# A graph network's first edge sweep: selections built from widened rows on TensorE, ScalarE and VectorE in place of products on VectorE and GpSimd

## The reference, cut to what matters

```python
xj = x[dst]                          # a row for each edge
s, v = xj[:, :64], xj[:, 64:]
msg  = linear(s, v)                  # plain
     + dist * mix(s, v)              # weighted by the fourth attribute
     + sum over i of r_vec[i] * mix_i(s, v)
agg  = segment_sum(msg, src)         # by the other end of the edge
x    = layernorm(x + x + bilinear(x, agg) + linear(x))
```

## Time and profile before

| | |
|---|---|
| median of 3 runs | 7056.59 us (7055.1 to 7059.43) |
| profiled execution, first to last instruction | 7384.0 us |
| sorting | to about 115 us |
| the first layer's sweep over the edges | about 115 to 2,482 us |
| first layer's node steps with the second layer's messages | about 2,500 to 5,410 us |
| second layer's node steps | to the end |
| busy over the whole span | PE 80%, PEld 64%, DVE 75%, ACT 51%, POOL 75% |

### The profile page before, as it was taken

One profiled execution on the slowest core, in us unless ns is written; L12 is line 12 of the kernel. 1 busy time (PEld: TensorE's weight loads), 2 busy tenths in 40 slices (PEclk: granted clock), 3 DMA queues, 4 the chain that ended last, 5 costly groups with the idle time before them and its releaser, 6 DMA issues.

```text
span 7384.0 us, 145782 instructions
## 1 busy us (share of the span) xinstructions
PE 5898.2 (80%) x52295; PEld 4739.6 (64%) x52295; DVE 5535.0 (75%) x7299; ACT 3742.5 (51%) x11578; POOL 5548.6 (75%) x4491
## 2 busy tenths in 40 slices
PE   5666666666666588888898989988849999999999
PEld 3444444545544477777776777777737777777777
DVE  5666666767666577777777777777728999998888
ACT  2232322323232355555555555555527777777776
POOL 3787877788878567777777777777757888888887
PEclk6777777777777799999999999999969999999999
DMA  7877777777776366776776777677632222222222
GB/s 219 244 229 223 230 218 224 224 225 232 224 221 194 107 203 229 234 234 222 232 242 223 239 237 228 227 236 231 211 118 93 94 94 94 94 94 95 95 96 75
DMA packets 681151, 1381.01 MB, mean 187 GB/s; under 512 B 106047, under 2 KB 487661, under 8 KB 654447
## 3 DMA queue, kind: packets, MB, share of 16 engines
q1 hardware_dynamic: 527695, 1090.23, 46.7%
q0 software_dynamic: 152736, 281.45, 11.3%
HBM read 587.20 MB, written 784.08 MB: 186 GB/s over the span
## 4 chain that ended last, share of the span: by engine, by line
PE 50%; DVE 13%; issue 12%; ACT 11%; another core or an unknown queue 8%; POOL 3%; SPq 1%; DMA 1%; DVEq 0%; POOLq 0%; ACTq 0%
PE node_ps L1373 13%; PE prods_ps L1341 5%; PE prods_ps L1322 5%; ACT onehot L1722 4%; PE prods_ps L1325 3%; DVE zs L1054 3%; PE node_ps L1390 3%; PE m_ps L1238 2%; PE s_ps L1238 2%; PE m_ps L1390 2%; POOL slots L649 2%; PE turn_ps L1360 2%; PE s_ps L1220 2%; PE node_ps L1238 2%
## 5 line engine op out<-in xcount | busy, mean ns | idle before, releaser
L649 POOL DMA_INDIRECT slots<-pay,slot_all x3136 | 3282.2, 1047 | 905.8 <-issue 835.5
L1722 ACT ACTIVATE onehot<-node_iota,msgs 128x125 f32<-128x125 f32 x3400 | 1030.2, 397 | 75.4 <-POOLq L711 75.4
L1373 PEld LDWEIGHTS node_ps<-msgs,onehot 128*125 128x125 f32 x6800 | 931.9, 188 | 149.3 <-issue 108.8
L1373 PE MATMUL node_ps<-msgs,onehot 128*125 128x160 f32 x6800 | 980.6, 303 | 45.8 <-ACT onehot L1728 32.7
L1104 DVE TENSOR_REDUCE upd<-work 125x48 f32<-125x3072 f32 x300 | 1003.9, 3346 | 6.9
L1091 DVE TENSOR_TENSOR work<-prods_ps,yv 125x1024 f32<-125x1024 f32 x800 | 930.9, 1216 | 35.6 <-PE prods_ps L1326 24.5
L1220 PE MATMUL s_ps<-ident,picks_sb 128*125 128x128 f32 x1568 | 377.2, 383 | 574.8 <-issue 486.3
L751 POOL TENSOR_TENSOR q<-xt,yv 125x3072 f32<-125x3072 f32 x100 | 547.7, 5477 | 339.6 <-PE turn_ps L1360 323.0
L1238 PE MATMUL m_ps<-win,picks_sb 125*128 125x160 f32 x3136 | 673.5, 343 | 104.7 <-issue 62.5
L724 POOL TENSOR_TENSOR q<-xt,yv 125x512 f32<-125x512 f32 x400 | 428.3, 1073 | 383.9 <-PE turn_ps L1360 360.7
L1220 PEld LDWEIGHTS s_ps<-ident,picks_sb 128*125 128x125 f32 x1568 | 306.4, 271 | 621.3 <-issue 610.2
(11 more groups left out here) (274 smaller groups left out, 14481.9 us busy)
## 6 DMA issues: line engine op xcount, KB each, us to landing
msgs<-slots SPq DMA_DIRECT2D x200, 1428.0 KB, 6.4
slots<-zero SPq DMA_DIRECT2D x183, 1386.0 KB
win<-table SPq DMA_DIRECT2D x784, 160.0 KB
picks<-picks_sb SPq DMA_DIRECT2D x196, 512.0 KB
picks_sb<-picks SPq DMA_DIRECT2D x196, 512.0 KB
table<-tab SPq DMA_DIRECT2D x200, 350.0 KB
slots<-pay,slot_all POOLq DMA_INDIRECT x3136
spill_in<-spill_sums SPq DMA_DIRECT2D x200, 80.0 KB, 6.0
```

Of the source, the lines that this page charges most:

```text
L649: g.indirect_dma_start(out=slots[layer][:, :], out_offset=bass.IndirectOffsetOnAxis(ap=slot_all[:, j:j + 1], axis=0), in_=pay[q][:, j - UB ...
L1373: te.matmul(node_ps[0:HM, 0:D], onehot[:, j, :], msgs[b][:, j, 0:D], start=(j == 0), stop=False)
L1722: last = ac.activation(onehot[:, j, :], node_iota[:, :], ACT.Square, bias=msgs[b][:, j, LOCAL:LOCAL + 1], scale=-1.0)
```

## The change

For each edge there are two rows now in SBUF, laid out with the edges along the free axis: the five weights (1, `dist`, r0, r1, r2; partitions 0 to 4 of `so.rows`) and `REL` (partition 32). `widen` multiplies them by constants, so that both appear on 125 partitions: `channel` (5 x 125) repeats each weight for the 25 nodes in `weight_ps`, a row of ones repeats `REL` in `s_ps`. ScalarE copies the weights to SBUF (`widened`), and one VectorE operation compares `REL` with the partition's own node and multiplies by the weight (`select`). The result is the turned selection itself, in `pick_n`; the transposes, `pick_out`, `weigh` and VectorE's two former operations are gone. All this is done one unit ahead, in halves of 4 blocks, and `select` stands within `rank_unit`, once in each half.

The attributes as rows are a new input (`attr_rows`, turned on the host); `REL` is turned piece by piece (`turn_rel` on TensorE, `keep_rel` on ScalarE), stored (`put_rel`), and loaded for each chunk (`load_rows`). The first layer's table matmuls now write to `turn_ps` and the second half of `prods_ps[1]`, since its first half holds the widened weights; `first_table` waits for `t_out` for that.

```diff
@@ sync @@
+            def put_rel(pc, groups, blocks):
+                sp.wait_ge(piece_out, 3 * pc + 3)
+                e0 = pc * PIECE * P
+                sp.dma_start(rel_d[e0:e0 + groups * blocks * P].rearrange("(g q e) -> q g e", q=blocks, e=P),
+                             so.rel_t[0:blocks, 0:groups, :]).then_inc(rel_put, 16)
             def load_recs(layer, k):
...
-                    if layer == 0:
-                        sp.wait_ge(s["picked"], 4 * c - 4)
-                        sp.wait_ge(s["weighed"], 4 * c - 4)
+            def load_rows(k):
+                c, ck, cb = k
+                if within(c, 2, NCH):
+                    sp.wait_ge(LS[0]["widened"], 4 * c - 4)
+                e0, n = c * CB * P, min(CB * P, E - c * CB * P)
+                sp.dma_start(so.rows[cb][1:CHANNELS, 0:n], attr_rows[:, e0:e0 + n]).then_inc(rows_in[cb], 16)
+                sp.dma_start(so.rows[cb][32:33, :].rearrange("p (a e) -> p a e", a=CB),
+                             rel_d[e0:e0 + CB * P].rearrange("(p a e) -> p a e", p=1, a=CB)).then_inc(rows_in[cb], 16)
...
             load_recs(0, (1, 0, 1))
+            sp.wait_ge(rel_put, 16 * (FULL + 1))
+            load_rows((0, 0, 0))
+            load_rows((1, 0, 1))
...
-                    sp.wait_ge(LS[0]["pick_out"], 4 * c + 2 * hh + 2)
+                    sp.wait_ge(LS[0]["picked"], 4 * c + 2 * hh + 2)
...
                 if within(c, 0, NCH - 2):
+                    load_rows(later(later(k)))
                     load_recs(0, later(later(k)))
@@ gpsimd @@
-            def weigh(k, hh, part):
...
             def chunk(k):
-                c, ck, cb = k
                 for hh in range(2):
-                    for part in range(2):
-                        if within(c, 0, NCH - 1):
-                            weigh(later(k), hh, part)
-                        scatter(0, k, hh, PAIRS // 2 * part, PAIRS // 2 * part + PAIRS // 2)
+                    scatter(0, k, hh)
@@ vector @@
-            def select(layer, k, hh):
...
+            def select(u, part):
+
+                c, hh, i = u // 2, u % 2, 2 * u + part
+                s, o = LS[0], UB // 2 * P * part
+                ve.wait_ge(s["wide_out"], i + 1)
+                if part == 0 and u >= 2:
+                    ve.wait_ge(s["msg"], 4 * u - 4)
+                    ve.wait_ge(picks_kept[hh], 16 * c)
+                ve.scalar_tensor_tensor(pick_n[hh][0:WROWS, o:o + UB // 2 * P], s_ps[0:WROWS, 0:UB // 2 * P], win_node[0:WROWS, :],
+                                        wide[part][0:WROWS, :], ALU.is_equal, ALU.mult).then_inc(s["picked"], 1)
...
                     link(ve.tensor_reduce(so.rank[:, hh, COUNT_COLS * pb:COUNT_COLS * (pb + 1)], pick, AX_X, ALU.add))
+                    if u + 1 < UNITS:
+                        select(u + 1, pb)
...
                     rank_unit(k, hh)
-                    if within(k[0], 0, NCH - 1):
-                        select(0, later(k), hh)
@@ tensor @@
+            def turn_rel(pc, groups, blocks):
+                te.wait_ge(edge_made, pc + 1)
+                rel = so.edge[:, :, :, :].rearrange("p c k f -> p (c k) f")[:, :, REL]
+                for g in range(groups):
+                    mm = te.transpose(s_ps[0:blocks, P * g:P * g + P], rel[:, blocks * g:blocks * g + blocks], ident[:, :])
+                mm.then_inc(turned_e, 1)
...
-            def turn_pick(layer, k, hh, part):
...
+            def widen(u, part):
+
+                c, hh, i = u // 2, u % 2, 2 * u + part
+                cb, s = c % 2, LS[0]
+                if i % 4 == 0:
+                    te.wait_ge(rows_in[cb], rows_first[cb] + 32 * (c // 2) + 32)
+                if i > 0:
+                    te.wait_ge(s["picked"], i)
+                o, n = UB * P * hh + UB // 2 * P * part, UB // 2 * P
+                te.matmul(weight_ps[0:WROWS, 0:n], channel[:, :], so.rows[cb][0:CHANNELS, o:o + n], start=True, stop=True)
+                te.matmul(s_ps[0:WROWS, 0:n], ones_f[32:33, 0:WROWS], so.rows[cb][32:33, o:o + n], start=True, stop=True
+                          ).then_inc(s["widened"], 1)
...
                 for hh in range(2):
-                    turn_pick(0, k, hh, 0)
+                    ahead = 2 * c + hh + 1
                     count(4 * c + 2 * hh + 1, 1)
-                    turn_pick(0, k, hh, 1)
                     messages(0, k, hh, 0, both)
+                    if ahead < UNITS:
+                        widen(ahead, 0)
                     if hh == 1 and made:
                         first_table(tile_of(k), 1)
                     messages(0, k, hh, 1, both)
...
                     messages(0, k, hh, 2, both)
+                    if ahead < UNITS:
+                        widen(ahead, 1)
                     messages(0, k, hh, 3, both)
@@ scalar @@
+            def keep_rel(pc, groups, blocks):
+                ac.wait_ge(turned_e, 2 * pc + 2)
+                if pc > 0:
+                    ac.wait_ge(rel_put, 16 * pc)
+                ac.copy(so.rel_t[0:blocks, 0:groups, :], s_ps[0:blocks, 0:groups * P].rearrange("q (g e) -> q g e", e=P)).then_inc(piece_out, 1)
...
-            def pick_out(layer, k, hh, part):
...
+            def widened(u, part):
+                i, s = 2 * u + part, LS[0]
+                ac.wait_ge(s["widened"], i + 1)
+                if i >= 2:
+                    ac.wait_ge(s["picked"], i - 1)
+                ac.copy(wide[part][0:WROWS, :], weight_ps[0:WROWS, 0:UB // 2 * P]).then_inc(s["wide_out"], 1)
...
                 for hh in range(2):
-                    pick_out(0, k, hh, 0)
-                    pick_out(0, k, hh, 1)
+                    ahead = 2 * c + hh + 1
                     located(0, k, hh)
                     pay_out(0, k, hh, 0, both)
+                    if ahead < UNITS:
+                        widened(ahead, 0)
...
                     pay_out(0, k, hh, 2, both)
+                    if ahead < UNITS:
+                        widened(ahead, 1)
                     pay_out(0, k, hh, 3, both)
```

More of the change, by code:

```diff
@@ L66 @@
 Q_MULS = (4, 1)
-MINE = 4
 DIRECT = (3, 2)
@@ L96, in layer_scales, with build @@
                 u_sv=(S * V) ** -0.5, u_vs=(S * V) ** -0.5)
-def build(nc, x, src, dst, attr, weights, out):
+def build(nc, x, src, dst, attr, attr_rows, weights, out):
     N = x.shape[0]
@@ L191, in build @@
         pick_n = pick_b[0:2]
-        pick_e = [z[:, 0:UB * WROWS].rearrange("p (j n c) -> p j n c", j=UB, c=CHANNELS) for z in pick_b[2:4]]
+        wide = [pick_b[2][:, z * UB // 2 * P:(z + 1) * UB // 2 * P] for z in range(2)]
         pay = [sb(f"pay{q}", [P, UB, ROW]) for q in range(4)]
@@ L246, in build @@
         so.zeros = sb("zero_rows", [P, ZERO * D], F32, early)
+        so.lane_i = sb("lane_i", [P, WIN], I32, early)
+        so.lane = sb("lane", [P, WIN], F32, early)
+        so.channel_i = sb("channel_i", [CHANNELS, WROWS], I32, early)
+        so.rel_t = pick_b[0][:, 0:PIECE].rearrange("q (g e) -> q g e", e=P)
+        so.rows = [z[0:33, :, :].rearrange("p g e -> p (g e)") for z in so.attr]
         early.close()
@@ L279, in build @@
             sem(z) for z in ("floats", "turned_e", "piece_out", "keyed", "based", "spread", "edge_made", "edge_put"))
+        rel_put = sem("rel_put")
+        rows_in, rows_first = piece_in[0:2], [48 * ((FULL + 1 - b) // 2) for b in range(2)]
         hot, counted, ranking, placed = sem("hot"), sem("counted"), sem("ranking"), sem("placed")
@@ L295, in layer_sems @@
                 s[n] = sem(f"{n}_l{layer}")
-            for n in (("picked", "weighed", "pick_turned", "pick_out"), ("copied", "mixed_mul"))[layer]:
+            for n in (("widened", "wide_out", "picked"), ("copied", "mixed_mul"))[layer]:
                 s[n] = sem(f"{n}_l{layer}")
@@ L971, in chunk @@
                     scale([(0, 1), (1, 0), (1, 1)])
-            ve.wait_ge(consts, 3)
+            ve.wait_ge(consts, 4)
             bucket_rows(0, 0)
-            select(0, (0, 0, 0), 0)
-            select(0, (0, 0, 0), 1)
+            for b in range(2):
+                one = ve.memset(so.rows[b][0:1, :], 1.0)
+            one.then_inc(consts, 1)
+            select(0, 0)
+            select(0, 1)
             chunk_sweep(ve, chunk)
@@ L1209, in count @@
                 mm.then_inc(counted, 1)
-            def turn_pick(layer, k, hh, part):
-                c, ck, cb = k
-                s = LS[layer]
-                te.wait_ge(s["picked"], 4 * c + 2 * hh + 2)
-                te.wait_ge(s["weighed"], 4 * c + 2 * hh + 2)
-                if within(2 * c + hh + part, 1, 2 * UNITS):
-                    te.wait_ge(s["pick_out"], 4 * c + 2 * hh + part)
-                for j in range(UB // 2):
-                    mm = te.transpose(s_ps[0:WROWS, P * j:P * j + P],
-                                      pick_e[hh][:, UB // 2 * part + j, :, :].rearrange("p n c -> p (n c)"), ident[:, :])
-                mm.then_inc(s["pick_turned"], 1)
+            def widen(u, part):
[9 more added lines that the diff above has]
```

(20 more changed lines are left out.)

79 lines of the change are left out of this document (36 added, 43 removed).

## The result

The changed kernel takes 7750.81 us (median of 4 runs) against 7058.01 us for the kernel before, measured beside it: a ratio of 1.098 (95% interval 1.0965 to 1.0996). It is 693 us slower; the prediction said 7300 us with a range up to 7620.

A forecast was written before the change was run, and what follows sets the result against it. GpSimd (POOL) was taken as the bound at 12.06 us a unit. Afterwards the ring, 2 x 4.40 + 2.00 = 10.8, plus 2.28 and 0.2 for the clock, gives 13.3; over 196 units +243 us, 7300 us (range 6880 to 7620).

The forecast's parts named there:

- What bounds the kernel now: First layer's edge sweep: GpSimd's scatters and `weigh` products fill 12.06 us a unit; removing the products saves 1.33 us.
- The ring: Each half unit: `bucket_rows`, `count`, `messages`, `widen`, copy, `select` and hand-overs in a row, 4.40 us at full clock.
- `place` chain: VectorE's small chained operations between `select` and `bucket_rows`, in one of a unit's two halves: 2.00 us.
- `widen` side by side: TensorE's two widening matmuls start together and take 1.12 us for the pair at full clock.
- The second rival: `widen`'s two matmuls run one after the other: 16.3 us a unit, +830 us, 7890 us; chance 0.12.
- The clock: TensorE in the sweep: half clock in one pass a unit adds 2.28 us, plus 0.2 us: 13.3 us a unit.
- the pass behind the gap: The pass after TensorE's 3.6 us idle stretch, once a unit, runs at half clock: 2.28 us more.
- The third rival: TensorE's clock stays low in both passes, as if thin matmuls held it: 15.4 us a unit, 7710 us; chance 0.08.
- The first rival: The clock holds or the ring is looser: 10.8 to 11.8 us a unit, 6810 to 7005 us; chance 0.25.
- The signs it named: Changed profile: `select` every 6.6 us, POOL idle over 2 us a unit, clock 0.7 to 0.8, `widen` matmuls starting together.
- Edges: Sweep's start costs 10 us for a second DRAM trip, its end saves some 10 us; they cancel.
- The 10 us hoped for at the end: End of the sweep: POOL trails TensorE by 17.5 us; without its backlog some 10 us go.

The follow-up runs named there:

- the removal alone: The kernel before, with GpSimd's `weigh` products removed and VectorE multiplying all eight blocks: 6802.31 us, ratio 0.9638.
- the ring open: The changed kernel with the one-hot of pass g+2 written once pass g is done with its buffer: 7060.47 us; with 64 and 64 rows too, 6844.56 us.

## Why the prediction was wrong

- **What bounds the kernel now** (GpSimd, 12.06 us a unit, 1.33 of it removable): right, and shown by taking the removal alone.
- **The ring** that the new wait closes: right, with its terms nearly to size. At half clock a pass from one `bucket_rows` to the next is 8.51 us less the `place` chain, 6.7; forecast 4.40 + 2.28 = 6.68. At full clock 4.51 against 4.40. Within it `select` took 0.75 (forecast 0.69), `messages` at full clock 0.70 to the start of the pair (0.54), the pair 1.06 to the next start (1.12), at half clock 1.32 and 2.01 (1.08 and 2.24).
- **`widen` side by side:** right; the pair starts within 0.01 us. The second rival's price was about right, its case did not occur.
- **The clock: the step that failed.** The prediction wrote that "the pass behind the gap [...] runs at half; the other pass is mostly at full, and I add 0.2 us". The gap and the low pass came as written, but the other pass was low as well, from end to end in one unit of two and in the other up to its pair (in the chunk shown; over the sweep the second passes in which the tables' matmuls stand ended with a pair at half clock in 67 of 98 chunks): 8.43 and 5.35 us, mean 6.89, in place of 4.6: +2.29 us a unit, of which the `place` passes (8.52 for 8.68) give 0.16 back. That is the 2.1 us between this chunk's 15.4 us a unit and the forecast's 13.3. The reason given, that 5.3 us of ordinary matmuls had brought the clock back in the earlier trace rows, did not carry over: those contract 125 to 128 rows, while in the ring a pass behind the gap spends 2.0 of its 4.6 us on the pair of 5 and 1 rows. With 64 and 64 rows the clock is the one forecast, and a unit takes 12.92 us (13.3 forecast), the kernel 7269.81 us (7300 forecast). The total is nearer than its terms: 0.38 us a unit is 74 us, and the misses at the edges took part of that back.
- The third rival named the mechanism, "as if the thin matmuls kept it from rising", with 15.4 us a unit (15.35 measured) and 7710 us (7751). That its number fits so well is partly luck: it had every second pass at 4.40 + 2.28 = 6.68 us, while one unit of two had 1.75 us more for the tables' matmuls, and the other 1.33 less because the clock came back before its pair. Its chance of 0.08 was too small, and the range left it out. The evidence held against it was a burst without any thin matmul, so it could not speak on the question.
- **A smaller miss in the same step:** the ring's sum had no term for the tables' matmuls. With 64 and 64 rows they nearly hide (5.06 us a pass on average over the sweep where they stand, 4.51 where they don't); at half clock they make a pass of 6.7 us one of 8.43, in every second unit, which is 0.9 of the 2.29 us.
- The first rival (the removed transposes lift the clock) did not occur: the clock fell when they went. By the rule of the Trainium skill that it cited (TensorE: Matmul & The Clock Gate, Part 4: PE-mode transpose), their going should not have lowered it. The runs don't isolate transposes, so whether the rule holds is open here. The matmuls that replaced them account for the fall: with 64 and 64 rows in them the clock is 0.80, above the 0.76 of before.
- **The signs it named:** `select` came every 7.7 us on average, not 6.6; As written, VectorE waited for ScalarE's copy, TensorE had one long gap a unit (3.15 us, and 2.54 in every second unit), and the pair started together. The clock was 0.58, not 0.7 to 0.8. GpSimd was idle for 7.5 us a unit, but the profile names no releaser for it (831.9 us of "issue"), so that it waited for ScalarE's copies is not shown.
- **Edges:** the start cost 21.5 us, not 10. TensorE's first pair waited 7.46 us for the second trip through DRAM, about as long as VectorE had waited for the first:

```profile
125.34 1.18 PE L1240 MATMUL prods_ps<-attr_n,channel 5*125 5x512 f32 x1 [7.46 <-DMA attr_n<-edge_rel]
```

The first pairs ran at half clock as well. The 10 us hoped for at the end did not come: GpSimd's last scatter still trails TensorE's last messages by 16.0 us (3139.68 to 3155.7) against 17.5. Together they are some 20 us.

## What to carry to other kernels

Before replacing an engine's operation, draw the round trip that the new one closes, through every engine's program order, and price it; the cheapest first edit is often the removal alone, which here gave 255 us. A matmul that contracts few rows takes as long as one with many (the pair 1.06 us at full clock with 5 and 1 rows as with 64 and 64) and, where it makes up much of TensorE's work, may leave everything around it at half clock: pad two side-by-side matmuls to the full array and look at the granted clock again. If one engine's order is changed to shorten a ring, the next engine's order must follow, or the work stays in it.

## What the runs showed of the hardware that was not expected

- The granted clock went with the rows of the array that the widening pair used: 0.58 with 5 and 1, 0.58 with 16 and 16, 0.61 with 32 and 32, 0.59 with 64 and 64 one behind the other; 0.80 with 64 and 64 side by side, 0.87 with 128 and 128. TensorE's gap before the pass behind it was the same with 5 and 1 as with 64 and 64 (3.15 and 3.17 us). The added rows had zero weights, so the kernel computed the same numbers in all these runs. Whether the columns of the array count as well was not tried.
- Matmuls of 64 and of 1 rows, on rows 0 to 63 and 64, did not run side by side, while 5 and 1, 16 and 16, 32 and 32, and 64 and 64 did.
- With the ring open and thin matmuls, TensorE was busy 459 of 500 us at a clock of 0.64; with 64 and 64 rows and the ring open it was busy 374 of 500 at 0.90.
